# A fused attention and expert kernel: steps moved within the slots of the row stage, one-hots built column by column, merged squares

## The reference, cut to what matters

```python
def _L0_xattn_ref(p, k_v, W_k, b_k, ln_gamma, ln_beta):
    kv = k_v @ W_k.T + b_k
    out = jnp.einsum('bij,bjd->bid', p, kv)
    sim = jnp.einsum('bid,bjd->bij', out, kv) * scale
    mu, var = jnp.mean(sim, axis=-1, keepdims=True), jnp.var(sim, axis=-1, keepdims=True)
    sim = (sim - mu) * jax.lax.rsqrt(var + EPS) * ln_gamma + ln_beta
    return jax.nn.softmax(sim, axis=-1)

def _L0_ffn_ref(x, Wg, W1, W2, W3):
    topk_s, topk_i = jax.lax.top_k(jnp.einsum('btd,ed->bte', x, Wg), 2)
    w = ...   # softmax of the two scores, spread over the 8 experts
    for e in range(8):
        h = silu(x @ W1[e].T) * (x @ W2[e].T)
        y = y + w[..., e:e + 1] * (h @ W3[e].T)
    return y
x = x + _L0_xattn_ref(_layernorm(x), ctx_512, ...)
x = x + _L0_ffn_ref(_layernorm(x), Wg, W1, W2, W3)
```

## Time and profile before

| | |
|---|---|
| median of three runs | 387.84 us (387.68 to 389.34) |
| the profiled execution | 388.07 us, of which the span from first to last instruction is 386.3 |
| busy share of the span | PE 92%, DVE 69%, ACT 69%, POOL 44% |
| row stage with routing | 0 to about 120 us |
| expert stage | about 120 to 380 us |
| mean granted TensorE clock | 0.967 |

### The profile page before, as it was taken

The page is one execution under the profiler, slowest core; times in us unless marked ns, Lnnn a source line. Parts: engine busy times, 40 slices in busy tenths (PEclk is TensorE's granted clock), DMA queues, the critical chain, the costliest instruction groups (busy, mean ns, idle before and its releaser), DMA issues.

```text
span 386.3 us, 8154 instructions
## 1 busy us (share of the span) xinstructions
PE 356.9 (92%) x2277; PEld 233.2 (60%) x2277; DVE 267.9 (69%) x661; ACT 268.2 (69%) x467; POOL 171.6 (44%) x202
## 2 busy tenths in 40 slices
PE   5999999998896778889999999999999999999981
PEld 4656676776653545556666666666666666666640
DVE  1268688857976999995757576666767575757660
ACT  1289999979696978976666657575666666666650
POOL 2124856659934135545253434344343435253331
PEclk9999999998776999999999999999999999999997
DMA  6999999999503123255544445353536354544423
GB/s 194 416 383 409 347 382 403 369 317 372 204 3 84 28 57 55 56 86 88 104 66 99 76 91 84 81 90 79 99 66 109 61 106 66 100 73 95 80 30 54
DMA packets 21945, 57.60 MB, mean 149 GB/s; under 512 B 4816, under 2 KB 4944, under 8 KB 20368
## 3 DMA queue, kind: packets, MB, share of 16 engines
q0 software_dynamic: 8736, 20.53, 29.6%
q1 hardware_dynamic: 12016, 30.27, 21.2%
q10 hardware_dynamic: 1152, 6.29, 4.6%
HBM read 38.17 MB, written 18.91 MB: 148 GB/s over the span
## 4 chain that ended last, share of the span: by engine, by line
PE 55%; DVE 6%; issue 4%; DMA 1%; ACT 1%; DVEq 1%; POOLq 0%; ACTq 0%
PE bank L1251 32%; PE bank L1285 17%; PE bank L1242 4%; PE bank L1271 3%; DVE stage L983 2%; DVE Wp L833 2%; DMA out<-kvj_s,sidx 1%; DVE x_s L1015 1%; DVE kvg_s L989 1%; ACT stage L677 1%; DVE n_s L1007 0%; POOLq L74 0%; DVE wsel L999 0%; DVEq L996 0%; DVE wmul L1003 0%
## 5 line engine op out<-in xcount | busy, mean ns | idle before, releaser
L983 DVE SCALAR_TENSOR_TENSOR stage<-W,w3sc,stage 128x512 f16<-128x512 f16 x117 | 84.2, 747 | 6.5 <-ACT stage L677 5.9
L1285 PE MATMUL bank<-stage,n_s 128*128 128x512 f16 (+1 forms) x351 | 82.2, 379 | 3.5 <-DVE n_s L1007 2.0
L1251 PE MATMUL bank<-Wp,kvg_s 128*128 x480 | 80.2, 318 | 4.8 <-DVE kvg_s L989 4.8
L677 ACT ACTIVATE stage<-W,w3sc 128x512 f16 x117 | 80.1, 717 | 0.0
L1251 PE MATMUL bank<-Wp,kv_s 128*128 x456 | 74.3, 313 | 2.0 <-DVE kv_s L989 2.0
L511 POOL DMA_INDIRECT out<-oT_s,sidx x20 | 34.2, 1712 | 75.9 <-ACT oT_s L704 68.7
L1251 PEld LDWEIGHTS bank<-Wp,kvg_s 128*128 128x128 f16 x480 | 47.5, 99 | 32.2 <-issue 6.7
L511 POOL DMA_INDIRECT out<-kvj_s,sidx x19 | 32.4, 1707 | 66.1 <-ACT kvj_s L704 63.5
L1251 PEld LDWEIGHTS bank<-Wp,kv_s 128*128 128x128 f16 x456 | 44.5, 98 | 26.6 <-issue 3.0
L1007 DVE TENSOR_TENSOR n_s<-bank,n_s 128x384 f16<-128x384 f32 x39 | 21.7, 557 | 55.3 <-ACT n_s L690 55.3
L1285 PEld LDWEIGHTS bank<-stage,n_s 128*128 128x128 f16 (+1 forms) x351 | 34.2, 98 | 36.7 <-issue 3.9
(11 more groups left out here) (189 smaller groups left out, 553.8 us busy)
## 6 DMA issues: line engine op xcount, KB each, us to landing
Wp<-in_w SPq DMA_DIRECT2D x8, 1408.0 KB, 11.2
W<-in_w ACTq DMA_DIRECT2D x8, 768.0 KB, 7.6
stage<-in_xT SPq DMA_DIRECT2D x4, 1024.0 KB, 8.2
W<-in_x SPq DMA_DIRECT2D x12, 256.0 KB, 8.6
out<-W SPq DMA_DIRECT2D x12, 256.0 KB, 9.5
n_table<-n_s SPq DMA_DIRECT2D x8, 256.0 KB, 7.6
n_table<-x_s SPq DMA_DIRECT2D x8, 256.0 KB, 6.3
stage<-in_x SPq DMA_DIRECT2D x4, 256.0 KB, 9.2
```

Source lines behind the costliest of these rows:

```text
L677: eng.activation(w3p[t % 2][:, c * D:(c + 1) * D], W3[:, bass.ds(e * W3N + c * D, D)], ACT.Copy, scale=w3sc[:, bass.ds(e, 1)]).then_inc(s_ ...
L983: eng.scalar_tensor_tensor(w3p[r][:, W3N + c * D:W3N + (c + 1) * D], W3[:, bass.ds(e * W3N + c * D, D)], w3sc[:, bass.ds(e, 1)], w3p[r][:, ...
L1251: mm = eng.matmul(bank[2 * which + r][:, 0:H], n_, w_, start=(c == 0 and k == 0), stop=(c == DC - 1 and k == 2))
L1285: mm = eng.matmul(ybank(t - 1)[:, :], h_, w_, start=(c == 0 and k == 0), stop=(c == HC - 1 and k == 2))
```

## The change

- **POOL**: `first_low` goes; DVE does that low part with its own instruction, `w12_low(0, 0)`, after the routing.
- **ACT**: the squares of W1 and W2 are one instruction of 2816 elements per expert, in every second slot. The copies of the turned rows g = 1, 3, ..., 11 go to DVE (`by_vector`), one slot later. `scaled` comes first in the slot, `kvj_evac` after `weigh`. `number` goes. `w12_high(0, 0)` comes after the last copy.
- **DVE**: `columns` builds each choice's two one-hots in instructions of their own, 128 contiguous elements each, with the values of r, q and the token number as per-partition operands, so the product with the token number is in the same instruction. There are 5 groups instead of 4 (three of four row groups and two of two); each is placed earlier by its own table of slots.
- **PE**: `turn_keys` moves behind `sims`, `gram_outs` behind `sims` and `outs`; `rank(0)`, `rank(1)` and `table(0)` are in slots 11, 14 and 15; a `table` matmul waits for its own column. The counts of `warm` change: 4 for 8 in slots up to 10, 8 for 12 in slots 11 to 13. The first rows are turned before W3's squares are summed.
- **SP**: the loads of ctx and wk are issued ahead of bk.

```diff
-WARM_GATHER = 20
+WARM_GATHER = 36
+WARM_ROWS = 10
 WARM_DRAIN = 6
-WARM_SLOT = 8
-WARM_LATE = 12
-WARM_START = 30
+WARM_SLOT = 4
+WARM_LATE = 8
+WARM_LAST = 12
+WARM_START = 55
+GROUPS = ((0, 4), (4, 4), (8, 4), (12, 2), (14, 2))
+NG = len(GROUPS)
...
+        def by_vector(g):
+            return g % 2 == 1 and g < G - TPB
+        def turned_ready(eng, g):
+            if by_vector(g):
+                eng.wait_ge(s_nTv, sum(by_vector(i) for i in range(g + 1)))
+            elif g >= 0:
+                eng.wait_ge(s_nT, sum(not by_vector(i) for i in range(g + 1)))
...
-            def first_low():
-                eng.wait_ge(s_hi, 1)
-                eng.tensor_scalar(wst[0][:, 0:WH], wst[0][:, 0:WH], wscale[:, 0:1], None, ALU.mult).then_inc(s_raw, 1)
-                eng.wait_ge(s_raw, 1)
-                eng.tensor_tensor(Wp[:, W12N:W12N + WH], wst[0][:, 0:WH], Wp[:, 0:WH], ALU.subtract).then_inc(s_lo, 1)
...
             def slot(s):
                 weight_loads(s)
-                if row(s - 4):
-                    turned(s - 4)
                 if row(s + 1):
                     scaled(s + 1)
-                if 0 <= s + 3 < 2 * E:
-                    squares((s + 3) // 2, (s + 3) % 2)
+                if row(s - 4) and not by_vector(s - 4):
+                    turned(s - 4)
+                if (s + 2) % 2 == 0 and 0 <= (s + 2) // 2 < E:
+                    squares((s + 2) // 2)
...
-            def squares(k, h):
+            def squares(k):
                 eng.wait_ge(s_w[k], 16)
-                wait(eng, s_wq, 2 * k + h)
-                eng.activation(wjunk, wst[k][:, h * WH:(h + 1) * WH], ACT.Square,
-                               accum_out=wsq[:, k, h:h + 1]).then_inc(s_wq, 1)
+                wait(eng, s_wq, k)
+                eng.activation(wjunk, wst[k], ACT.Square, accum_out=wsq[:, k:k + 1]).then_inc(s_wq, 1)
...
                 ring_free(eng, q)
-                cols, ring = slice(g0 * TOPK, (g0 + m) * TOPK), slice(i0, i0 + m * TOPK)
-                shape = [P, P, m * TOPK]
-                eng.wait_ge(s_rqf, 2 * q + 1)
-                eng.tensor_tensor(oh_r[:, a, :, ring], steps8[:, :, ring], rf[:, None, cols].to_broadcast(shape), ALU.is_equal).then_inc(s_ohp, 1)
                 eng.wait_ge(s_rqf, 2 * q + 2)
-                eng.tensor_tensor(oh_c[:, a, :, ring], steps8[:, :, ring], qf[:, None, cols].to_broadcast(shape), ALU.is_equal).then_inc(s_ohc, 1)
...
+                for c in range(m * TOPK):
+                    n, g = g0 * TOPK + c, g0 + c // TOPK
+                    eng.tensor_scalar(oh_r[:, a, i0 + c, :], ramp[:, 0, :], rf[:, n:n + 1], tok1[:, g:g + 1],
+                                      ALU.is_equal, ALU.mult).then_inc(s_ohr, 1)
+                    eng.tensor_scalar(oh_c[:, a, i0 + c, :], ramp[:, 0, :], qf[:, n:n + 1], None, ALU.is_equal).then_inc(s_ohc, 1)
...
+            def turned(g):
+                eng.wait_ge(s_nTp, g + 1)
+                eng.wait_ge(s_scp, g + 1)
+                eng.tensor_copy(nT_s[:, g % 2, :], bank[6][:, :]).then_inc(s_nTv, 1)
...
+                if s == 12:
+                    places(0)
+                if s == 14:
+                    columns(0)
                 if s == 15:
-                    places(0)
+                    places(1)
                 if s == 16:
                     weight_scale()
-                    columns(0)
+                    columns(1)
...
             eng.wait_ge(s_et, 1)
-            eng.wait_ge(s_lo, 1)
+            w12_low(0, 0)
             w12_low(0, 1)
             low_rows(0)
```

More of the change, by code:

```diff
@@ L479, in _ @@
             router_gap(2)
-            first_low()
             router_weights(0)
@@ L588, in slot @@
                     weigh(s + 1)
+                b = batch_at(s, 3, 2)
+                if b is not None:
+                    kvj_evac(b)
                 b = batch_at(s, 0, 1)
@@ L605, in w3_square @@
                 eng.activation(w3junk[k > 1], W3[:, e * W3N:(e + 1) * W3N], ACT.Square, accum_out=w3sq[:, e:e + 1]).then_inc(s_w3q, 1)
-            def number(q):
-                eng.wait_ge(s_ohp, q + 1)
-                for i in range(TPB):
-                    cols = slice(i * TOPK, (i + 1) * TOPK)
-                    eng.activation(oh_r[:, q % 2, :, cols], oh_r[:, q % 2, :, cols], ACT.Copy,
-                                   scale=tok1[:, q * TPB + i:q * TPB + i + 1]).then_inc(s_ohn, 1)
             def router_exp(part):
@@ L653, in _ @@
             turned(G - 3)
-            number(0)
             turned(G - 2)
@@ L877, in slot @@
                     centre_keys(b)
+                if row(s + 2):
+                    x_stats(s + 2)
                 b = batch_at(s, 2, 1)
@@ L880, in slot @@
                     gram_copy(b)
+                if row(s - 5) and by_vector(s - 5):
+                    turned(s - 5)
                 if row(s - 6):
@@ L918, in _ @@
                 slot(s)
-            places(1)
             chosen(G - 4)
-            columns(1)
+            places(2)
             chosen(G - 3)
-            places(2)
-            chosen(G - 2)
-            columns(2)
-            chosen(G - 1)
             classes(3)
             class_sums(3)
+            columns(2)
+            chosen(G - 2)
+            places(3)
+            chosen(G - 1)
+            classes(4)
+            class_sums(4)
+            columns(3)
             steps = [0]
@@ L936, in then @@
                 eng.wait_ge(s_r, steps[0])
-            places(B - 1)
-            columns(B - 1)
+            places(NG - 1)
+            columns(NG - 1)
             eng.wait_ge(s_cntp, 1)
@@ L1037, in _ @@
             tabled = []
-            wide = steps8[:, :, :].rearrange("p a c -> p (a c)")[:, 0:3 * P]
+            wide = ramp[:, :, :].rearrange("p a c -> p (a c)")
             def warm(moving, times, home=5):
@@ L1192, in slot @@
                 if b is not None:
-                    outs(b)
+                    turn_keys(b)
                 if row(s - 3):
                     turn_n(s - 3)
+                if b is not None:
+                    outs(b)
+                b = batch_at(s, 1, 1)
+                if b is not None:
+                    gram_outs(b)
                 if s == 13:
                     weight_norms()
+                if s == 15:
+                    table(0)
             eng.wait_ge(s_const, 1)
@@ L1218, in _ @@
             turn_n(G - 2)
+            rank(2)
             router(G - 3)
[L1220 removed]
             turn_n(G - 1)
             router(G - 2)
[L1223 to L1224 removed]
             table(1)
             rank(3)
+            router(G - 1)
+            table(2)
+            rank(4)
             counts()
[L1228 to L1229 removed]
             table(3)
+            warm(wide, WARM_DRAIN // 2)
+            table(4)
             eng.wait_ge(s_sel, 1)
```

142 lines of the change are left out of this document (57 added, 85 removed).

## The result

The changed kernel takes 400.69 us (median of 4 runs, 399.35 to 402.24), the kernel before 388.53 on the same chip: ratio 1.0324, interval 1.029 to 1.0358. It is 12 us slower. The forecast was 382.8 us with a range up to 387.5, and it was wrong in sign.

A forecast was written before the change was run, and what follows sets the result against it. It took PE as the bound in the row loop and DVE before the steady tiles; -3.9 + 1.9 - 1.15 - 0.8 - 0.6 - 0.5 = -5.05 us gave 382.8 against the median, range 379.8 to 387.5.

The forecast's parts named there:

- I let these cancel: Row loop on PE: later gram product and batch 0's msq against the earlier ctx load, together priced at nothing.
- I put 0.5 to 2 us of new PE waits there and take 1.1.: Row loop, tightest batch: PE would wait for turned rows copied a slot later on DVE, costing 1.1 us.
- -3.1 - 1.95 for the thinner filler: Row loop: fewer constant matmuls on a full PE, 3.1 us from 14 slots and 1.95 from slots 11 to 13.
- -2.6 for whole squares and -2.8 for copies off ACT "must follow": Row loop: ACT work saved by whole squares and six fewer copies, so that ACT keeps up with PE's faster pace.
- The row loop's -3.9: Sum of the PE part in the row loop: -5.0 from fewer constant matmuls, plus 1.1 of new waits.
- One-hots 14.4 us: Routing on DVE: 32 pairs of narrow instructions at 0.45 us each, range 12.5 to 18.6, replacing 5.4 us.
- The stretch: Routing: DVE's stretch grows from 27.4 to 29.3 us, +1.9; its wait for the last table goes, -1.15.
- -0.8 to the first tile: From 113.07 to 120.02 us: ACT's W3 squares end before the gather lands, taking 0.8 off 6.95 us.
- -0.6: Start of tile 0: DVE's 0.59 us wait for ACT's high part goes, as ACT makes it before the rows arrive.
- The slower one: Routing: narrow DVE instructions wait for POOL and pairs cost 0.58 us, giving 390.2 us; chance 0.12.
- Rival 2: Row loop held by DMA, ACT or late DVE copies: first part worth 1 instead of 3.9, 385.7 us; chance 0.15.
- The sign that the text gave for being wrong: Row loop: PE was to stay without a gap; PE waits for DVE's copies would make the 1.1 us wrong.

The follow-up runs named there:

- b_pe: The kernel before with the change's PE order and ACT's second key evacuation behind the spread and weighing, nothing else: 394.25 us, ratio 1.0146.
- b_pe_act: The kernel before with the change's PE order and ACT's two edits (scaling ahead of turned copies, whole squares): 399.05 us, ratio 1.0264.
- u_pe: The changed kernel with PE's row-loop order put back, and ACT's second key evacuation ahead of the spread: 389.94 us, ratio 1.0050.
- k_fill: k_half with 8 constant matmuls in each slot again, 12 in slots 11 to 13: 387.94 us, ratio 1.0008.
- u_copy: The changed kernel with all turned copies on ACT again, nothing else: 401.34 us, ratio 1.0333.
- k_half: u_all with the filler behind the index product at 20 matmuls for 36, squares in halves: 386.38 us, ratio 0.9934 to the kernel before.
- k_merge: k_half with each expert's weights squared whole in every second slot: 387.39 us, ratio 0.9968.
- k_copy: k_half with the odd turned copies on DVE: 388.60 us, ratio 1.0019.
- u_half: The changed kernel with each expert's weights squared again in two halves in two slots, nothing else: 396.77 us, ratio 1.0220.
- u_all: The changed kernel with the whole row loop put back; thinner filler, early loads, narrow one-hots, five groups and DVE's first low half stay: 386.97 us, ratio 0.9976.

## Why the prediction was wrong, step by step

- **"The gram product now stands behind `sims` and, at the start, the msq of batch 0 comes one `sims` later; ... I let these cancel."** This is the step that failed: the reordering was put at nothing. It priced the moved PE steps by their own length, and never asked who waits for the results; the key turns and outs have no term at all. The move alone costs 5.7 us (b_pe), with ACT's two edits 10.2 (b_pe_act), and undoing it in the changed kernel gave back 10.7 (u_pe). The early loads, which I let cancel too, were real: `outs(0)` 2.8 us sooner. In k_fill, with the filler and the order of before, 1.1 of that are left at the end of the row loop (81.71 for 82.79).
- **"I put 0.5 to 2 us of new PE waits there and take 1.1."** The waits were put on the copies on DVE, which cost nothing more in the changed kernel (u_copy). The longest waits of PE were for ACT's copies: 1.84 in the changed kernel, and 2.19 in b_pe, where the swap with scaling is not in it. The swap makes them later still: undone, it gave back 5.0.
- **-3.1 - 1.95 for the thinner filler.** Oversized: 2.6 to 2.9 on the good order (k_fill against k_half). ACT is busy all 15 of 15 us from 60 to 75 in k_half, which fits a loop that ACT holds in part; nothing isolates it.
- **-2.6 for whole squares and -2.8 for copies off ACT "must follow".** They were not counted again in the sum, but were taken as help. On the old order they are +1.3 and +3.3 us (k_merge, k_copy). In the changed kernel the whole squares are 4.1 of the loss (u_half), and the copies nothing that can be told (u_copy).
- **The row loop's -3.9.** With the old order it ends 3.5 us earlier (u_all, 79.25 against 82.79). That the size came out there is luck: the filler gave 2.6 for the 5.0 of the sum, the earlier start 1.1 where it had been let cancel, and the 1.1 of new waits was put on copies that u_all does not have.
- **One-hots 14.4 us.** In u_all the 32 pairs take 13.1 (five groups: 3.09, 3.81, 3.13, 1.55, 1.55), 0.386 a pair undisturbed and 0.41 on the mean: below the 0.45 I took and near the low bound. The Trainium skill's rule ("VectorE: DVE Perf Modes", the TRN2 errata) gave an estimated 12.2; undisturbed it would be 12.4, so on the mean the trace agrees with the page. The single steps are 0.22 us with two per-partition operands and 0.16 with one. **The stretch** (+1.9 - 1.15 = +0.75 to the table) measured +0.8 in u_all: 31.08 us from the sum of squares to the table read back, against 30.28. In the changed kernel itself it is 32.36, +2.1, so this term failed there too. Even in u_all its parts did not match: 1.3 less for the pairs, and waits that I had given 0.7, the longest for PE's ranks, 1.39. In u_all:

```profile
79.25 0.17 DVE L801 TENSOR_REDUCE wsum<-bank 128x8 f32<-128x16 f32 x1 [0.74 <-PE bank L1146]
...
97.17 0.22 DVE L773 TENSOR_TENSOR pick<-oh,bank 128x64 f32<-128x64 f16 x1 [1.39 <-PE bank L1068]
...
110.33 0.28 DVE L955 CAST tabT<-bank 128x128 f16<-128x128 f32 x1
...
117.88 0.69 DVE L992 SCALAR_TENSOR_TENSOR kvg_s<-bank,kvg_s 128x512 f16<-128x512 f32 x1 [1.58 <-ACT kvg_s L666]
```

- **-0.8 to the first tile, and "the longer filler lies in the gather's wait".** Wrong: the 36 matmuls took 6.37 us and ended at 130.0, when gather plus 3.7 is 128.2. From the table to the low rows it was 7.92 us against 6.95, a loss of 1.0; with the old row loop it was 7.55 (u_all), and with 20 matmuls 6.48 (k_half), a gain of 0.5. **-0.6** for DVE's wait behind `low_rows` came true (no wait at 131.92, 0.59 before). **-0.5** for the ramp did not: 49.64 against 49.56 us, though the granted clock rose from 0.94 to 0.97.
- **The rivals.** The slower one, narrow instructions behind POOL, is small: single ones held 0.3 to 0.4 us each. Rival 2, a row loop that does not speed up, had the right place but half the courage: it was bounded at a gain of 1, with nothing below nothing. None named a circle of waits. The sign that the text gave for being wrong, PE with gaps in the row loop, is what the profile showed.

## What to carry to other kernels

In a software pipeline where three engines are nearly level, price a moved step by its consumer: for each result that it issues later, name the instruction on the other engine that takes it, and follow one batch round until it comes back to the step. If two or three engines move at once, the delays can close into a circle: here the moves on PE cost 5.7 us, whole squares 1.3 on the old order, and both with the swap on ACT 10.2 (the swap was not run alone). The sign was that all engines' busy shares fell together. Test such edits one engine at a time, and size a filler behind which real work stands at the slower clock.

## What the runs showed that I had not expected

A filler meant to hold the clock ran itself below full clock: 36 matmuls of 256 columns took 6.37 us, 0.177 each, and 20 took 4.43 in k_half, 0.22 each, where 20 took 2.34 before, 0.117 each; the granted clock in those stretches was 0.62, 0.50 and 1.00. It starts behind a wait of PE of 1.6 us for the table read back (0.5 before). And more filler is no safeguard: b_pe_act has 8 matmuls in each slot and fell to 0.66 between 60 and 75 us, with its eight matmuls of outs at 6.12 us; u_pe has 4 and stayed at 1.00, with PE busy 9.0 and 8.8 of 10 us. The Trainium skill ("TensorE: Matmul & The Clock Gate", Part 1) says that the clock follows how busy PE has been, which agrees with these rows.
